# A hybrid attention block on one Trainium2 core: receptance of the first FFN from an input mixed beforehand, residual sums on GpSimd

## The chip, the core and the metric

The kernel runs on one core of a Trainium2 chip. The core has five engines that work side by side, each through its own queue of instructions in the order in which the program gave them: TensorE (PE in the profile, with PEld for the loading of its weights), VectorE (DVE), ScalarE (ACT), GpSimd (POOL) and SyncE (SP), which only issues transfers here. They wait for each other through semaphores. The metric is the device time of one execution in microseconds (us). The kernel before took 864.21 us in the median of three runs (862.68 to 866.72).

## The reference

The input x is (2, 2048, 128), all of it float32. Four parts follow each other, each as x = x + part(layernorm(x)): an attention, a feed-forward part (FFN), a linear attention with a decaying state, and the same FFN again. The change concerns the first FFN. Its computation, with C = 128 and the layernorm's output called x:

```
x_prev = concatenate([zeros, x[:, :-1, :]], axis=1)      # the token before
xr = mu_r * x + (1 - mu_r) * x_prev                      # mu_r, mu_k: one number per channel
xk = mu_k * x + (1 - mu_k) * x_prev
r  = sigmoid(xr @ W_r)                                   # receptance
k  = xk @ W_k
out = r * (square(relu(k)) @ W_v)
```

The result `out` is added to the stream that entered the layernorm.

## The kernel before

The stream X stays in SBUF through the whole kernel: 32 tiles of 128 tokens by 128 channels. The first FFN is the function `ffn_phase` (lines 775 to 984). It works on 8 groups of 4 tiles (512 tokens), which alternate between the two sequences of the batch. Group g of one sequence uses buffer `g.b`, so each tile has two buffers. Each engine runs a loop of its own over 10 slots (`run_slots`); `g.later(k)` is the group k places further on, and `exists` says whether there is one. The order inside `slot` is the order in which an engine's queue is filled. Nothing in it is reordered later. In slot g:

- VectorE: normalize group g+1 (four instructions, line 112), moments of group g+2 (line 94 and line 99), output of group g-2: `gated = (tanh + 1) * o` from PSUM (line 872) and then the residual sum into X (line 874).
- GpSimd: `low_part` of group g (line 848), the part of x that its rounded copy `x_hi` leaves out; then the inverse roots of group g+2 (lines 105 and 107), which the normalization of that group waits for.
- ScalarE: copy of the transposed x out of PSUM (line 904) and its rounded copy `x_hi` (line 906) for group g; then tanh (line 911), relu (line 916) and square (line 919) for group g-1. In slots 0, 1, 6 and 7 tables of the linear attention are computed there too.
- TensorE: transposes of group g (`turn`, line 947), receptance of group g-1 (lines 965 and 966), values of group g-2 (line 973), keys of group g-1 (lines 955 to 957).

After the transposition channels lie on the partitions, so "the token before" is the column to the left. `xT` has 1 + 512 columns, the first being the last one of the group before. The mixing with mu is not applied to x. It is in the weights: `FfnWeights.vector` makes two scaled copies of W_r and of W_k in the attention phase, and each product is done twice, once with x and once with x shifted by a column, into the same PSUM sum. The last FFN, which is woven into the end of the linear attention by another class (`LastFfn`), does the same and uses the same weights.

A `Block` ends when all engines have run through their part of it. The attention's block lies before the FFN's, the linear attention's behind it. In the last slots VectorE and GpSimd also compute the first normalization of the linear attention (`first_moments`, `first_gpsimd`, `first_normalized`).

Of the kernel before, what the change touches and what calls it, by code (L numbers as in the profile page):

```python
# [17 lines left out]
ALU = mybir.AluOpType  # L18
ACT = mybir.ActivationFunctionType
AX = mybir.AxisListType  # L20

P = 128
B, T, C = 2, 2048, 128
NT = T // P
GT = 4
G = GT * P
# [748 lines left out]
def ffn_phase(nc, X, const, weights, norm, name, out=None, tables=None, next_norm=None):  # L775


    normed = 2
    wr, wk_hi, wk_lo, wv = weights.wr, weights.wk_hi, weights.wk_lo, weights.wv
    ctx = ExitStack()  # L780
    with ctx:
        sb = lambda what, shape, dt=F32: ctx.enter_context(nc.sbuf_tensor(name + what, shape, dt))
# [4 lines left out]
        xT = sb("xT", [P, 2, 1 + G])  # L787
# [3 lines left out]
        k_act = sb("k_act", [P, 2, G])  # L791
        r_tanh = sb("r_tanh", [P, 2, G])
        gated = sb("gated", [P, 2, G])
        xt_ps = [psum(f"xt_ps{b}") for b in range(2)]
        k_ps = [psum(f"k_ps{b}") for b in range(2)]
        r_ps = [psum(f"r_ps{b}") for b in range(2)]
        o_ps = [psum(f"o_ps{b}") for b in range(2)]

        (set_up, xt_full, carried, xt_ready, hi_ready, lo_ready, k_full, k_pos_ready, k_act_ready, r_full, r_ready, o_full,
         gated_ready, x_ready, stored) = (sem(n) for n in (  # L800
             "set_up", "xt_full", "carried", "xt_ready", "hi_ready", "lo_ready", "k_full", "k_pos_ready", "k_act_ready",
             "r_full", "r_ready", "o_full", "gated_ready", "x_ready", "stored"))
        GROUPS = B * NG

        def run_slots(eng, slot):

            for k in range(GROUPS + 2):  # L810
                slot(Tile(0, k))

        AHEAD = 2

        def exists(g):
            return not isinstance(g.m, int) or 0 <= g.m < GROUPS

        def late(g):

            return not isinstance(g.m, int) or g.m >= 2  # L820

        def has_been_normed(g):
            return isinstance(g.m, int) and g.m < normed

        def tokens(g):
            return X[:, bass.ds(g.b * NT + g.n * GT, GT), :]
# [3 lines left out]
        @block.sync  # L830
        def _(eng):
            if tables is not None:
                tables.sync(eng)
            if out is not None:
                for k in range(GROUPS):
                    g = Tile(0, k)
                    eng.wait_ge(x_ready, k + 1)
                    eng.dma_start(out[g.b, g.n * G:(g.n + 1) * G, :].rearrange("(t p) c -> p t c", p=P),
                                  X[:, g.b * NT + g.n * GT:g.b * NT + (g.n + 1) * GT, :]).then_inc(stored, 16)
                eng.wait_ge(stored, 16 * GROUPS)  # L840

        @block.gpsimd
        def _(eng):
            eng.memset(xT[:, :, 0:1], 0.0).then_inc(set_up, 1)

            def low_part(g):
                eng.wait_ge(hi_ready, g.count(1, 1))
                eng.tensor_tensor(x_lo[:, g.b, :], xT[:, g.b, :], x_hi[:, g.b, :].bitcast(F32), ALU.subtract).then_inc(lo_ready, 1)

            def slot(g):  # L850
                if exists(g):
                    low_part(g)
                if exists(g.later(2)):
                    norm.inverse_roots(eng, g.later(2))
                if next_norm is not None and g.off == GROUPS - 2:
                    next_norm.first_gpsimd(eng)

            run_slots(eng, slot)

        @block.vector  # L860
        def _(eng):
            eng.sem_inc(gated_ready, AHEAD)

            def normalize(g):
                if late(g):
                    eng.wait_ge(xt_full, g.count(1, -1))
                norm.normalize(eng, g)

            def output(g):
                eng.wait_ge(r_ready, g.count(1, AHEAD + 1))  # L870
                eng.wait_ge(o_full, g.count(1, AHEAD + 1))
                eng.scalar_tensor_tensor(gated[:, g.b, :], r_tanh[:, g.b, :], 1.0, o_ps[g.b][:, :], ALU.add, ALU.mult).then_inc(gated_ready, 1)
                eng.wait_ge(gated_ready, g.count(1, AHEAD + 1))
                eng.tensor_tensor(tokens(g), gated[:, g.b, :].rearrange("p (t c) -> p t c", t=GT), tokens(g), ALU.add).then_inc(x_ready, 1)

            def slot(g):
                if next_norm is not None and g.off == GROUPS - 1:
                    next_norm.first_normalized(eng)
                if exists(g.later(1)) and not has_been_normed(g.later(1)):
                    normalize(g.later(1))  # L880
                if exists(g.later(2)):
                    norm.moments(eng, g.later(2))
                if exists(g.later(-2)):
                    output(g.later(-2))
                if next_norm is not None and g.off == GROUPS - 2:
                    eng.wait_ge(x_ready, B)
                    next_norm.first_moments(eng)

            run_slots(eng, slot)

        @block.scalar
        def _(eng):
            eng.sem_inc(r_ready, AHEAD)
            eng.sem_inc(k_pos_ready, AHEAD)
            eng.wait_ge(set_up, 1)
            def copy_x(g):
                eng.wait_ge(xt_full, g.count(1, 1))
                if late(g):

                    eng.wait_ge(k_full, g.count(1, -1))  # L900
                    eng.wait_ge(r_full, g.count(1, -1))
                    eng.activation(xT[:, g.b, 0:1], xT[:, g.b, G:G + 1], ACT.Copy).then_inc(carried, 1)
                    eng.wait_ge(carried, g.count(1, -1))
                eng.activation(xT[:, g.b, 1:1 + G], xt_ps[g.b][:, :], ACT.Copy).then_inc(xt_ready, 1)
                eng.wait_ge(xt_ready, g.count(1, 1))
                eng.activation(x_hi[:, g.b, :], xT[:, g.b, :], ACT.Copy).then_inc(hi_ready, 1)

            def tanh(g):
                eng.wait_ge(r_full, g.count(1, 1))
                eng.wait_ge(gated_ready, g.count(1, AHEAD - 1))  # L910
                eng.activation(r_tanh[:, g.b, :], r_ps[g.b][:, :], ACT.Tanh, scale=0.5).then_inc(r_ready, 1)

            def square(g):

                eng.wait_ge(k_full, g.count(1, 1))
                eng.activation(k_pos[:, g.b, :], k_ps[g.b][:, :], ACT.Relu).then_inc(k_pos_ready, 1)
                eng.wait_ge(k_pos_ready, g.count(1, AHEAD + 1))
                eng.wait_ge(o_full, g.count(1, AHEAD - 1))
                eng.activation(k_act[:, g.b, :], k_pos[:, g.b, :], ACT.Square).then_inc(k_act_ready, 1)

            def slot(g):
                if exists(g):
                    copy_x(g)
                if exists(g.later(-1)):
                    tanh(g.later(-1))
                    square(g.later(-1))
                if tables is not None and isinstance(g.m, int):
                    if g.m < 2:
                        tables.scalar_heads(eng, range(g.m * H // 2, (g.m + 1) * H // 2))
                    elif GROUPS - 2 <= g.m < GROUPS:  # L930
                        half = g.m - (GROUPS - 2)
                        tables.scalar_pairs(eng, range(half * NP // 2, (half + 1) * NP // 2))
                    elif g.m == GROUPS:
                        tables.scalar_rest(eng)

            run_slots(eng, slot)

        @block.tensor
        def _(eng):
# [18 lines left out]
                mm.then_inc(k_full, 1)  # L958

            def receptance(g):  # L960
                eng.wait_ge(xt_ready, g.count(1, 1))
                eng.wait_ge(r_ready, g.count(1, AHEAD - 1))
                for j in range(GT):
                    ps = r_ps[g.b][:, j * P:(j + 1) * P]
                    eng.matmul(ps, xT[:, g.b, 1 + j * P:1 + (j + 1) * P], wr[:, 0, :], start=True, stop=False)
                    mm = eng.matmul(ps, xT[:, g.b, j * P:(j + 1) * P], wr[:, 1, :], start=False, stop=True)
                mm.then_inc(r_full, 1)

            def values(g):
# [6 lines left out]
            def slot(g):  # L976
                if exists(g):
                    turn(g)
                if exists(g.later(-1)):
                    receptance(g.later(-1))  # L980
                if exists(g.later(-2)):
                    values(g.later(-2))
                if exists(g.later(-1)):
                    keys(g.later(-1))
# [1312 lines left out]
```

## Time and profile before

| | |
|---|---|
| median of three runs | 864.21 us (862.68 to 866.72) |
| the profiled execution's own time | 863.95 us |
| its span | 862.0 us, granted TensorE clock 0.984 |
| PE busy | 804.1 us (93%) |
| DVE busy | 550.2 us (64%) |
| ACT busy | 557.5 us (65%) |
| POOL busy | 562.2 us (65%) |
| first FFN's block in the trace | from 208.7 us to 252.2 us |

The span is the time between the first and the last instruction in the profile; the execution's own time is a little longer. A row of the timeline gives the start and the duration of one or several merged instructions, the engine, the line, the tile written and the tiles read. What stands in brackets is the time in which the engine was idle ahead of it and whom it waited for. The duration of an instruction that has started and can't proceed contains what it is held up.

### The profile page before, as it was taken

Reading aid. Unit: us, or ns where it says so; the run is one execution under the profiler, and the core shown is the slowest. Engines: PE = TensorE matmul, PEld = TensorE weight load, DVE = VectorE, ACT = ScalarE, POOL = GpSimd, SP = SyncE. Lnnn points to the kernel's source line nnn. Section 1 sums busy time; section 2 is a strip of 40 time slices with the busy share of each in tenths; the row PEclk is TensorE's granted clock in tenths of the full one; section 3 lists DMA queues with packets and bytes.
Section 4 is the critical chain, followed back from the end, with each engine's and each line's share of the span. In section 5 each row is a group of like instructions: output and inputs, shape, how many; then the busy total and the mean of one; then the engine's idle time right before and its main releaser. Section 6 shows DMA issues by size and latency. Waiting matters only on the chain.

```text
span 862.0 us, 31084 instructions
## 1 busy us (share of the span) xinstructions
PE 804.1 (93%) x13187; PEld 697.9 (81%) x13187; DVE 550.2 (64%) x1267; ACT 557.5 (65%) x1171; POOL 562.2 (65%) x449
## 2 busy tenths in 40 slices
PE   5879999998978999999999999999999999987886
PEld 4668998897967878888888878888788898786776
DVE  5997567566853665666666646656665667566573
ACT  5755555554768667677767766776777677754544
POOL 5961111214538888798797797797887977976431
PEclk9999999999989999999999999999999999998999
DMA  4300000100000000000000000000000000000011
GB/s 143 109 1 19 25 19 14 26 13 14 15 2 2 3 2 3 4 3 3 3 4 2 2 5 2 2 4 3 3 3 2 4 3 2 5 3 2 14 37 49
DMA packets 20423, 12.36 MB, mean 14 GB/s; under 512 B 7872, under 2 KB 19008, under 8 KB 20288
## 3 DMA queue, kind: packets, MB, share of 16 engines
q1 hardware_dynamic: 20288, 10.39, 4.3%
q8 instruction: 105, 1.72, 0.8%
q14 instruction: 30, 0.25, 0.1%
HBM read 8.29 MB, written 2.10 MB: 12 GB/s over the span
## 4 chain that ended last, share of the span: by engine, by line
PE 52%; ACT 6%; POOL 5%; DVE 4%; issue 3%; ACTq 0%; POOLq 0%; DVEq 0%
PE la_ps L1465 8%; PE la_ps L1467 6%; PE la_ps L1466 6%; PE la_o_ps L1528 4%; PE la_o_ps L1544 4%; PE la_s_ps L1558 4%; PE la_ps L1575 3%; PE la_ps L1509 3%; ACT la_u_hi L1960 2%; PE la_ps L1496 2%; PE la_ps L1610 2%; PE la_ps L1611 2%; PE la_ps L1612 2%; ACT n_xn L2000 2%; POOL la_scale L2151 1%
## 5 line engine op out<-in xcount | busy, mean ns | idle before, releaser
L2119 POOL TENSOR_TENSOR la_coef<-la_ssk,lt_mhalf 128x32 f32<-128x32 f32 x16 | 87.0, 5440 | 72.3 <-DVE la_ssk L1788 72.3
L1465 PE MATMUL la_ps<-la_x_hi,w_hi 128*128 128x256 f32 x384 | 116.8, 304 | 2.0 <-ACT la_v L1930 1.0
L1466 PE MATMUL la_ps<-la_x_lo,w_hi 128*128 128x256 f32 x384 | 107.6, 280 | 0.2 <-issue 0.2
L1467 PE MATMUL la_ps<-la_x_hi,w_lo 128*128 128x256 f32 x384 | 107.7, 280 | 0.0
L2151 POOL TENSOR_TENSOR la_scale<-la_scale,lt_mhalf 128x32 f32<-128x32 f32 x16 | 97.8, 6110 | 5.3 <-DVE la_scale L1764 5.2
L1811 DVE TENSOR_TENSOR lt_state<-la_s_ps,la_faded 128x512 f32<-128x512 f32 x62 | 42.6, 687 | 69.9 <-PE la_o_ps L1544 46.5
L1465 PEld LDWEIGHTS la_ps<-la_x_hi,w_hi 128*128 128x128 f32 x384 | 72.2, 188 | 14.3 <-issue 6.2
L524 POOL CAST w_hi<-qkv_w_raw 128x256 fp32r<-128x256 f32 x20 | 7.9, 396 | 115.0 <-PE qkv_xt_ps L566 78.9
L593 PE MATMUL qkv_v_ps<-V,qkv_probsT 128*128 128x128 f32 x544 | 72.0, 279 | 2.6 <-DVE qkv_probsT L507 1.6
L593 PEld LDWEIGHTS qkv_v_ps<-V,qkv_probsT 128*128 128x128 f32 x544 | 67.9, 192 | 7.4 <-ACT qkv_probsT L697 2.5
L1466 PEld LDWEIGHTS la_ps<-la_x_lo,w_hi 128*128 128x128 f32 x384 | 72.5, 189 | 0.8 <-issue 0.4
L1467 PEld LDWEIGHTS la_ps<-la_x_hi,w_lo 128*128 128x128 f32 x384 | 72.3, 188 | 0.0
L1951 ACT ACTIVATE la_gate<-la_ps,lt_bias_g 128x256 f32<-128x256 f32 x128 | 50.0, 482 | 33.1 <-PE la_ps L1467 33.1
L2145 POOL TENSOR_TENSOR la_faded<-lt_state,lt_decay_s 128x512 f32<-128x512 f32 x62 | 64.1, 1043 | 2.2 <-DVE lt_state L1811 2.2
L1748 DVE TENSOR_TENSOR la_pT<-la_ps,lt_decay 128x512 f32<-128x512 f32 x64 | 41.0, 683 | 38.1 <-PE la_ps L1509 38.1
L2137 POOL TENSOR_TENSOR la_k<-la_k,lt_decay_k 128x1024 f32<-128x1024 f32 x32 | 60.9, 1904 | 2.0 <-issue 1.1
L2129 POOL TENSOR_TENSOR la_v<-la_v,la_coef 128x1024 f32<-128x1024 f32 x32 | 60.2, 1903 | 1.3
L1951 ACT ACTIVATE la_f<-la_ps,lt_bias_f 128x256 f32<-128x256 f32 x128 | 51.5, 472 | 14.7 <-PE la_ps L1467 13.3
L689 ACT ACTIVATE qkv_probs<-qkv_xt_ps,at_ntop 128x512 f32<-128x512 f32 (+3 forms) x48 | 30.4, 633 | 46.8 <-DVE at_ntop L630 46.8
L1465 PE MATMUL la_ps<-w_hi,la_x_hi 128*128 128x512 f32 x128 | 57.4, 448 | 0.0
L1930 ACT ACTIVATE la_k<-la_ps 128x512 f32<-128x512 f32 x64 | 38.3, 598 | 26.3 <-PE la_ps L1467 23.3
L1544 PE MATMUL la_o_ps<-la_qdT,lt_state 64*64 64x64 f32 x2048 | 46.1, 224 | 8.4 <-issue 5.0
(225 smaller groups left out, 2439.3 us busy)
## 6 DMA issues: line engine op xcount, KB each, us to landing
qkv_w_raw<-in_w SPq DMA_DIRECT2D x20, 128.0 KB, 2.2
X<-in_x SPq DMA_DIRECT2D x8, 256.0 KB, 2.9
out<-X SPq DMA_DIRECT2D x8, 256.0 KB, 2.3
qkv_cos<-in_cos SPq DMA_DIRECT2D x4, 256.0 KB, 3.1
qkv_sin<-in_sin SPq DMA_DIRECT2D x4, 256.0 KB, 3.9
lt_w_out<-in_w_out SPq DMA_DIRECT2D x4, 128.0 KB, 2.7
qkv_w<-in_w_qkv SPq DMA_DIRECT2D x1, 320.0 KB, 3.2
const<-in_const SPq DMA_DIRECT2D x1, 256.5 KB, 5.3
```

The source lines that it names most:

```text
L593: mm = eng.matmul(o_ps[n % 2][:, 0:P], probsT[:, (BLK[n] + j) % 2, t * P:(t + 1) * P], V[:, bass.ds(b * NT + kt, 1), :], start=(kt == 0), ...
L1465: eng.matmul(out, l_hi, r_hi, start=True, stop=False)
L1466: eng.matmul(out, l_hi, r_lo, start=False, stop=False)
L1467: return eng.matmul(out, l_lo, r_hi, start=False, stop=True)
L1544: mm = eng.matmul(o_ps[h % 2][rows, part(i, c)], state[own, b, h // 2, :], qdT[own, b, h // 2, chunk(c)], start=False, stop=True, skip_gro ...
L1811: eng.tensor_tensor(state[:, b, :, :], s_ps[c][:, :].rearrange("p (r e) -> p r e", r=NP), faded[:, b, :, :], ALU.add).then_inc(up_read[c], 1)
L1951: act = eng.activation(where[:, c, :], ps[bank][:, r * W:(r + 1) * W], ACT.Tanh, bias=bias[:, c:c + 1], scale=0.5)
L2119: eng.tensor_tensor(coef[:, :], ssk[:, :], mhalf[:, :], ALU.pow).then_inc(s["coef_step"], 1)
L2129: eng.tensor_tensor(own, own, over_d(coef[:, b * H:(b + 1) * H]), ALU.mult).then_inc(s["vb_ready"], 1)
L2137: eng.tensor_tensor(own, own, over_d(decay_k[:, :]), ALU.mult).then_inc(s["kd_ready"], 1)
L2145: eng.tensor_tensor(faded[:, b, :, :], state[:, b, :, :], over_e, ALU.mult).then_inc(s["faded_second" if c else "faded_first"], 1)
L2151: eng.tensor_tensor(scale[:, :, :], scale[:, :, :], powers, ALU.pow).then_inc(s["scale_step"], 1)
```

## The change

The receptance gets its mixed input, `xr = mu_r * x + (1 - mu_r) * x_prev`, computed ahead of the product. ScalarE multiplies x by mu_r with one more instruction per group (`own_ready`), and VectorE adds the shifted x times (1 - mu_r) with one `scalar_tensor_tensor` (`mix`, between the normalization and the moments of a slot). TensorE then does the receptance's product once, with the unscaled weights. The residual sum moves from VectorE's `output` to the end of GpSimd's slot (`residual`), and `output` waits until the residual sum two groups back has read `gated`. The last FFN stays as it is.

```diff
-    wr, wk_hi, wk_lo, wv = weights.wr, weights.wk_hi, weights.wk_lo, weights.wv
+    wk_hi, wk_lo, wv = weights.wk_hi, weights.wk_lo, weights.wv
...
+        xr = sb("xr", [P, 2, G])
...
+            def residual(g):
+                eng.wait_ge(gated_ready, g.count(1, AHEAD + 1))
+                eng.tensor_tensor(tokens(g), gated[:, g.b, :].rearrange("p (t c) -> p t c", t=GT), tokens(g), ALU.add).then_inc(x_ready, 1)
+
             def slot(g):
                 if exists(g):
                     low_part(g)
                 if exists(g.later(2)):
                     norm.inverse_roots(eng, g.later(2))
+                if exists(g.later(-2)):
+                    residual(g.later(-2))
                 if next_norm is not None and g.off == GROUPS - 2:
                     next_norm.first_gpsimd(eng)
...
             def output(g):
                 eng.wait_ge(r_ready, g.count(1, AHEAD + 1))
                 eng.wait_ge(o_full, g.count(1, AHEAD + 1))
+                if late(g):
+                    eng.wait_ge(x_ready, g.count(1, -1))
                 eng.scalar_tensor_tensor(gated[:, g.b, :], r_tanh[:, g.b, :], 1.0, o_ps[g.b][:, :], ALU.add, ALU.mult).then_inc(gated_ready, 1)
-                eng.wait_ge(gated_ready, g.count(1, AHEAD + 1))
-                eng.tensor_tensor(tokens(g), gated[:, g.b, :].rearrange("p (t c) -> p t c", t=GT), tokens(g), ALU.add).then_inc(x_ready, 1)
+
+            def mix(g):
+
+                own = xr[:, g.b, :]
+                eng.wait_ge(own_ready, g.count(1, 1))
+                eng.scalar_tensor_tensor(own, xT[:, g.b, 0:G], weights.rest[:, 0:1], own, ALU.mult, ALU.add).then_inc(xr_ready, 1)
 
             def slot(g):
                 if next_norm is not None and g.off == GROUPS - 1:
                     next_norm.first_normalized(eng)
                 if exists(g.later(1)) and not has_been_normed(g.later(1)):
                     normalize(g.later(1))
+                if exists(g):
+                    mix(g)
                 if exists(g.later(2)):
                     norm.moments(eng, g.later(2))
                 if exists(g.later(-2)):
...
                 eng.activation(x_hi[:, g.b, :], xT[:, g.b, :], ACT.Copy).then_inc(hi_ready, 1)
+                eng.activation(xr[:, g.b, :], xT[:, g.b, 1:1 + G], ACT.Copy, scale=weights.mu[:, 0:1]).then_inc(own_ready, 1)
...
             def receptance(g):
-                eng.wait_ge(xt_ready, g.count(1, 1))
+                eng.wait_ge(xr_ready, g.count(1, 1))
                 eng.wait_ge(r_ready, g.count(1, AHEAD - 1))
                 for j in range(GT):
-                    ps = r_ps[g.b][:, j * P:(j + 1) * P]
-                    eng.matmul(ps, xT[:, g.b, 1 + j * P:1 + (j + 1) * P], wr[:, 0, :], start=True, stop=False)
-                    mm = eng.matmul(ps, xT[:, g.b, j * P:(j + 1) * P], wr[:, 1, :], start=False, stop=True)
+                    part = slice(j * P, (j + 1) * P)
+                    mm = eng.matmul(r_ps[g.b][:, part], xr[:, g.b, part], weights.w[:, 0, :], start=True, stop=True)
                 mm.then_inc(r_full, 1)
```

## Rows read from the trace of the kernel before

**Rows 1.** The page, busy time by engine over the span
```profile
PE 804.1 (93%) x13187; PEld 697.9 (81%) x13187; DVE 550.2 (64%) x1267; ACT 557.5 (65%) x1171; POOL 562.2 (65%) x449
```
**Rows 2.** Timeline, PE: first transposes, then one slot (start us, duration us)
```profile
208.86 1.07 PE L947 MATMUL f_xt_ps<-const,n_xn 128*128 128x128 f32 x8 [0.87 <-PEq L147]
...
229.52 0.79 PE L947 MATMUL f_xt_ps<-const,n_xn 128*128 128x128 f32 x4
230.15 0.40 PE L965 MATMUL f_r_ps<-fw_wr,f_xT 128*128 128x128 f32 x2
...
231.95 1.06 PE L973 MATMUL f_o_ps<-fw_wv,f_k_act 128*128 128x128 f32 x8
...
234.22 0.77 PE L947 MATMUL f_xt_ps<-const,n_xn 128*128 128x128 f32 x4
```
**Rows 3.** Timeline, VectorE in the same slot
```profile
227.89 2.04 DVE L112 TENSOR_SCALAR n_xn<-X,n_mv,n_rstd 128x128 f32<-128x128 f32 x4 [0.17 <-POOL n_rstd L107]
229.85 0.86 DVE L94 BATCH_NORM_STATS2 n_stats<-X 128x6 f32<-128x128 f32 x4
...
231.74 0.69 DVE L874 TENSOR_TENSOR X<-f_gated,X 128x512 f32<-128x512 f32 x1
232.60 2.00 DVE L112 TENSOR_SCALAR n_xn<-X,n_mv,n_rstd 128x128 f32<-128x128 f32 x4 [0.17 <-POOL n_rstd L107]
```
**Rows 4.** Timeline, GpSimd in the same slot
```profile
227.79 1.29 POOL L848 TENSOR_TENSOR f_x_lo<-f_xT,f_x_hi 128x513 fp32r<-128x513 f32 x1
231.21 0.20 POOL L105 TENSOR_TENSOR n_rstd<-n_mv,n_eps 128x4 f32<-128x4 f32 x1 [2.13 <-DVE n_mv L99]
231.49 1.01 POOL L107 TENSOR_TENSOR n_rstd<-n_rstd,n_mhalf 128x4 f32<-128x4 f32 x1
232.46 1.29 POOL L848 TENSOR_TENSOR f_x_lo<-f_xT,f_x_hi 128x513 fp32r<-128x513 f32 x1
```
**Rows 5.** Timeline, the first and the last of the slot's four normalizing instructions
```profile
227.89 1.27 DVE L112 TENSOR_SCALAR n_xn<-X,n_mv,n_rstd 128x128 f32<-128x128 f32 x1 [0.17 <-POOL n_rstd L107]
...
229.59 0.34 DVE L112 TENSOR_SCALAR n_xn<-X,n_mv,n_rstd 128x128 f32<-128x128 f32 x1
```
**Rows 6.** Groups by line between 206 and 258 us: receptance, first product
```profile
L965 PE MATMUL f_r_ps<-fw_wr,f_xT 128*128 128x128 f32 x64 | 12.5, 278 | 0.3 <-ACT f_xT L904 0.3
```
**Rows 7.** Timeline, ScalarE: the rounded copy, and the wait for the keys
```profile
231.73 0.63 ACT L906 ACTIVATE f_x_hi<-f_xT 128x513 fp32r<-128x513 f32 x1
...
234.42 0.60 ACT L916 ACTIVATE f_k_pos<-f_k_ps 128x512 f32<-128x512 f32 x1 [1.56 <-PE f_k_ps L957]
```
**Rows 8.** Timeline, attention stage: GpSimd and VectorE, all with two SBUF inputs
```profile
52.70 1.29 POOL L254 TENSOR_TENSOR qkv_rot<-qkv_by_cos,qkv_by_sin 128x512 f32<-128x512 f32 x1
53.95 1.75 POOL L254 TENSOR_TENSOR qkv_rot<-qkv_by_cos,qkv_by_sin 128x512 f32<-128x512 f32 x1
...
52.73 1.81 DVE L298 TENSOR_TENSOR qk_lo<-qkv_rot,qk_hi 128x512 fp32r<-128x512 f32 x1
```
**Rows 9.** Timeline, GpSimd at the start of the first FFN
```profile
210.94 1.28 POOL L848 TENSOR_TENSOR f_x_lo<-f_xT,f_x_hi 128x513 fp32r<-128x513 f32 x1 [2.17 <-ACT f_x_hi L906]
...
212.46 1.03 POOL L107 TENSOR_TENSOR n_rstd<-n_rstd,n_mhalf 128x4 f32<-128x4 f32 x1
```
**Rows 10.** Timeline, the first FFN's end: VectorE, then PE
```profile
243.38 1.55 DVE L112 TENSOR_SCALAR n_xn<-X,n_mv,n_rstd 128x128 f32<-128x128 f32 x2 [0.33 <-POOL n_rstd L107]
...
251.19 0.69 DVE L874 TENSOR_TENSOR X<-f_gated,X 128x512 f32<-128x512 f32 x1
...
247.45 0.40 PE L957 MATMUL f_k_ps<-f_x_lo,fw_wk_hi 128*128 128x512 f32 x1
...
249.20 1.16 PE L973 MATMUL f_o_ps<-fw_wv,f_k_act 128*128 128x128 f32 x8 [1.35 <-ACT f_k_act L919]
```
**Rows 11.** Windows: stretch, PE, PEld, DVE, ACT, POOL busy us, then the granted clock
```profile
56.00:60.00 4.00, 1.99 (x12) 1.47 (x12) 3.79 (x12) 1.58 (x5) 2.41 (x2) 1.00 0.00 0
60.00:64.00 4.00, 3.34 (x15) 3.06 (x16) 3.79 (x14) 2.70 (x8) 0.00 (x0) 0.57 0.02 4
```

More of the change, by code:

```diff
@@ L797, in ffn_phase @@
         o_ps = [psum(f"o_ps{b}") for b in range(2)]
-        (set_up, xt_full, carried, xt_ready, hi_ready, lo_ready, k_full, k_pos_ready, k_act_ready, r_full, r_ready, o_full,
+        (own_ready, xr_ready, set_up, xt_full, carried, xt_ready, hi_ready, lo_ready, k_full, k_pos_ready, k_act_ready, r_full, r_ready, o_full,
          gated_ready, x_ready, stored) = (sem(n) for n in (
-             "set_up", "xt_full", "carried", "xt_ready", "hi_ready", "lo_ready", "k_full", "k_pos_ready", "k_act_ready",
+             "own_ready", "xr_ready", "set_up", "xt_full", "carried", "xt_ready", "hi_ready", "lo_ready", "k_full", "k_pos_ready", "k_act_ready",
              "r_full", "r_ready", "o_full", "gated_ready", "x_ready", "stored"))
```

## The prediction

> **What bounds the kernel now.** The page comes first: PE is busy for 93% of the span, the other engines for about 65% [rows 1]. Taken alone that says "PE bound", and the change takes PE work away. So the question for the first FFN is whether PE sets its pace there. I read the timeline of one slot, engine by engine, and look at which end a start follows.
>
> On PE a slot lasts from 229.52 to 234.22, 4.70 us, without idle time [rows 2]. Of that the receptance takes 231.95 - 230.15 = 1.80 us, values and keys 234.22 - 231.95 = 2.27 us, and the four transposes 230.15 - 229.52 = 0.63 us. Eight unhindered transposes took 1.07 us, of which the last one's duration is about 0.27, so one follows another after (1.07 - 0.27)/7 = 0.114 us and four need 0.46 us [rows 2]. The slot's transposes are therefore stretched by 0.17 us: they are waiting for something. The last normalizing instruction ends at 229.59 + 0.34 = 229.93 [rows 5], and the receptance starts 0.22 us behind it. A busy PE hides a wait of its own.
>
> What VectorE waits for is in [rows 3, 4]. It goes round in a loop with GpSimd, which needs nobody else:
> - the roots of a group end at 227.79 (GpSimd's next instruction starts there);
> - normalization 227.89 to 229.93. Unhindered it would be four instructions at 0.26 us. But GpSimd started `low_part` at 227.79 and VectorE's first instruction is held until this has nearly ended: 1.27 us instead of 0.34 [rows 5];
> - moments 229.85 to 231.13, roots 231.21 to 231.49 + 1.01 = 232.50, and VectorE starts on the next group at 232.60.
> From 227.79 to 232.50 is 4.71 us, the same as PE's slot, with only the short handovers between the engines in it. So the pace is set by this loop; PE, with 4.07 + 0.46 = 4.53 us of work, is close behind. The old residual sum (0.69 us) lies beside the roots [rows 3, 4], off the loop.
>
> **The change, part by part.**
> *Removed from PE.* Line 965 has 64 instructions in the eight groups, line 966 as many; a slot's receptance goes from 1.80 to 0.90 us, 7.2 us in all [rows 2, 6]. In the steady slots it is worth at most nothing, since the loop does not contain PE. It would count where PE is the path, in the tail (below).
> *Added on ScalarE.* One 128x512 copy with a scale; the nearest row is the rounded copy, 0.63 us, after which the next instruction starts 0.54 us on. ScalarE is idle for 1.56 us per slot waiting for the keys [rows 7], which hides it: 0, at worst 0.54 us a slot. It delays tanh, relu and the squares of the group before, for which PE has time once it is no longer close to the bound.
> *Moved off VectorE.* The residual sum, 0.69 us beside the roots: 0 on the loop.
> *Added on VectorE.* `mix` stands between normalization and moments, so it is on the loop. The nearest row for 128x512 with two SBUF inputs is 0.69 us [rows 3]; as the next instruction starts 0.60 us after it, I take 0.60. Bounds: 0.54 (the copy's step on ScalarE) and 1.81, the same shape held by a GpSimd instruction [rows 8]. The unhindered one is the nearer, as GpSimd has run out of streaming work when `mix` comes.
> *Added on GpSimd.* The residual sum of group g-2 stands right behind the roots of g+2 and ahead of `low_part` of g+1. Nearest rows: 1.29 us for the same size [rows 4, 8]. Its input is ready, because `output` runs beside the roots. So GpSimd starts it the moment the roots end, while VectorE starts 0.10 us later and finds it running. Two streaming instructions of GpSimd now come one after the other where there was one, and normalization has to wait for both. How they take turns is in [rows 8]: VectorE's 52.73 instruction was held by GpSimd's 52.70, ran when that ended, and GpSimd's next (53.95) was held for 1.75 - 1.29 = 0.46 us. So one normalizing instruction gets in between the two.
>
> *Sum of the loop.* 4.71 + 1.25 (residual sum) + 0.15 (the second GpSimd instruction held by a normalizing one) - 0.26 (that one is done already) + 0.60 (mix) = 6.45 us; if none gets in between, 4.71 + 1.28 + 0.60 = 6.59. I take 6.5, +1.8 per slot. Residual sums exist from slot 2 on. Before that a slot costs 4.71 + 0.60 = 5.3.
>
> The trace and the Trainium skill (SBUF — State Buffer, Who interferes with whom) can be weighed here. It says that the shared port pair is held for a whole instruction and that the loser blocks fully. By that a normalization held at 227.89 would end a full 0.34 + 3 x 0.26 = 1.12 us after `low_part`'s 229.08, at 230.20; the row says 229.93. With the page's version two collisions of 0.27 us a slot would come on top, about 2 us in all. The measurement decides; the sum goes by the rows. Another sentence of that section agrees with rows 8 and speaks against `mix`: a VectorE instruction with two SBUF inputs collides too.
>
> *Start.* `mix` of group 0 now stands ahead of the moments of group 2. It waits for ScalarE's two copies and is then held by `low_part` (210.94 + 1.28 = 212.2 [rows 9]): ends 212.8, moments 214.0, roots 215.35, against 212.46 + 1.03 = 213.5 before: +1.9. Roots of group 3: 215.35 + 5.3 = 220.7; group 4: 226.0; then 6.5 each: group 5 at 232.5, group 6 at 239.0, group 7 at 245.5. Before, group 7's were at 237.2 (232.50 and one more slot of 4.7). That is +8.3.
>
> *Tail.* Normalization of group 7 ends 3.3 instead of 2.1 us behind its roots: +9.5, at 248.8. Then mix, output and the linear attention's first moments on VectorE (the residual sum's 0.6 gone, mix's 0.6 added), but their roots must pass the residual sum of group 4 on GpSimd, some 0.6 us: the last first-normalized tile, before at 243.38 + 1.55 = 244.93 [rows 10], comes at 255.0. `mix` of group 7 is queued behind it, 255.6, and only now can PE do receptance, values and keys: 0.90 + 2.27 + 0.15 = 3.3 us, 258.9 instead of 247.45 + 0.40 = 247.85. That is +11.0; here PE's saved 0.90 us is already counted. From there relu, square, values and output as before, and a residual sum of 1.29 instead of 0.69 us [rows 10]: +11.6.
>
> *The clock.* PE now rests about 3 us per slot (6.5 - 3.6), in one piece, behind its keys. In the attention stage a window with 1.99 of 4 us busy was followed by one at granted clock 0.57 [rows 11], that is, most of it at the lower level of 1.2 GHz. In the steady slots PE has room for half speed over some 3.5 us. In the tail it hasn't: keys of group 6 end at about 252.7, PE then rests until 255.6, and the 3.3 us behind it may be done at half speed for most of their length: bounds 0 and +3.3, I take 1.3. Nothing behind the first FFN changes; its block starts as late as this one ends.
>
> Total: 11.6 + 1.3 = +12.9 us. The profiled execution took 863.95 us, 0.26 under the median, so 876.8 by its own time and **877.0 us** against the median.
>
> **The rivals.**
> *A: PE sets the pace.* For it: no idle time in the slot [rows 2] and 93% [rows 1]. Then 8 x 0.90 = 7.2 us go: 857. Against: the stretched transposes and the 0.22 us behind normalization in each slot.
> *B, not slower: the collisions don't add up.* If GpSimd's two streaming instructions ran beside the moments and beside VectorE's waits, the loop would be 0.10 + 1.03 + 0.60 + 1.28 + 0.08 + 1.29 = 4.4 us, 0.3 under today's. Six slots give -1.8, the receptance in the tail up to -1.8, the start +1.2 and the longer last sum +0.6: about 862.5. It decides if the residual sum is released later than the start of normalization. For it: the order of queueing between two engines is only read from rows of another stage. Against: `gated` is ready 0.8 us before the roots end.
> *C: only one of the two collides.* VectorE, once it has the port, gets all four and mix through ahead of `low_part`: 1.25 + 1.03 + 0.60 + 1.28 + 0.08 + 1.29 = 5.5 us per slot. The last three slots are 1.0 shorter each and the tail about 1: 873.
> *D: the clock makes PE the bound.* At half speed throughout, a slot's 3.6 us of PE become 7.3 (6.5 before): +0.8 x 4 slots and the tail's 3.3 in full: 882. Against: a PE that is busy throughout doesn't lose its clock [rows 11].
>
> **How the numbers follow.** The forecast has 0.55, C 0.20, D 0.10, A 0.05, B 0.10. The forecast's own range is 873 to 880; with C and D it is 869 to 882, which leaves out A, B and a rest. A measurement of this kernel can tell about 0.5% (4.3 us) from no change. Slower by more than that (above 868.5): forecast, C and D, 0.85. Within: B, and a rest of C, 0.10 less the part of B that goes further down, taken as 0.09. Faster: A and that part, 0.06.
>
> **What would show it.** In the profile after: the distance between two inverse roots (line 107 of `n_rstd`) in the middle of the first FFN is 6.4 to 6.6 us (forecast), 5.5 (C), 4.4 (B) or below 4.0 (A). The first normalizing instruction of a slot lasts about 1.3 us, and the second one too. GpSimd's residual sum starts within 0.1 us of the roots' end. PE shows 3 us idle a slot, with the clock at times at 0.5, and DVE as the releaser of the receptance. The block ends at about 265 instead of 252. It would be wrong if roots came at an even 4.7 us or less, or if the stages behind the first FFN took another time than before.

## The result, and the profile after

The changed kernel takes 880.8 us in the median of four runs (880.06 to 882.02), the kernel before 864.36 us beside it: ratio 1.0189, 95% interval 1.0167 to 1.021, or 16.4 us slower. The forecast was 877.0. The profiled execution took 880.06 us, its span is 878.0.

The loop of VectorE and GpSimd that stands in [rows 3, 4] comes first, since the forecast rests on it. GpSimd in the changed kernel, one slot and the next one's start:

```profile
226.57 1.28 POOL L853 TENSOR_TENSOR X<-f_gated,X 128x512 f32<-128x512 f32 x1
227.81 1.27 POOL L849 TENSOR_TENSOR f_x_lo<-f_xT,f_x_hi 128x513 fp32r<-128x513 f32 x1
231.62 0.20 POOL L105 TENSOR_TENSOR n_rstd<-n_mv,n_eps 128x4 f32<-128x4 f32 x1 [2.54 <-DVE n_mv L99]
231.90 1.02 POOL L107 TENSOR_TENSOR n_rstd<-n_rstd,n_mhalf 128x4 f32<-128x4 f32 x1
232.89 1.27 POOL L853 TENSOR_TENSOR X<-f_gated,X 128x512 f32<-128x512 f32 x1
```

And VectorE in the same slot, each normalizing instruction by itself; the last row is `mix`:

```profile
226.71 1.22 DVE L112 TENSOR_SCALAR n_xn<-X,n_mv,n_rstd 128x128 f32<-128x128 f32 x1 [0.90 <-POOL n_rstd L107]
227.86 1.31 DVE L112 TENSOR_SCALAR n_xn<-X,n_mv,n_rstd 128x128 f32<-128x128 f32 x1
229.09 0.34 DVE L112 TENSOR_SCALAR n_xn<-X,n_mv,n_rstd 128x128 f32<-128x128 f32 x1
229.34 0.33 DVE L112 TENSOR_SCALAR n_xn<-X,n_mv,n_rstd 128x128 f32<-128x128 f32 x1
229.60 0.74 DVE L887 SCALAR_TENSOR_TENSOR f_xr<-f_xT,fw_rest,f_xr 128x512 f32<-128x512 f32 x1
```

The residual sum starts the moment the roots end, the first normalizing instruction 0.14 us later is held by it until 227.93, and the second one is held by `low_part` until 229.17. In [rows 5] only the first was held. From one start of the residual sum to the next (226.57 to 232.89) it is 6.32 us, against 4.71 before.

PE in that slot; before, this stretch had no gap at all [rows 2]:

```profile
228.08 0.30 PE L963 MATMUL f_xt_ps<-const,n_xn 128*128 128x128 f32 x1 [0.54 <-DVE n_xn L112]
229.22 0.84 PE L963 MATMUL f_xt_ps<-const,n_xn 128*128 128x128 f32 x3 [0.84 <-DVE n_xn L112]
230.40 1.16 PE L981 MATMUL f_r_ps<-fw_w,f_xr 128*128 128x128 f32 x8 [0.33 <-DVE f_xr L887]
```

Together PE rests for 1.71 us of the slot, in three pieces, and part of its wait is hidden in the transposes, which take longer than where they run free.

The first FFN's start and end. The start: `mix` of group 0 on VectorE (1.25 us, held by `low_part`) and the receptance that waited for it. The end: the last residual sum, and ScalarE's first instruction in the linear attention's block:

```profile
211.59 1.25 DVE L887 SCALAR_TENSOR_TENSOR f_xr<-f_xT,fw_rest,f_xr 128x512 f32<-128x512 f32 x1 [3.11 <-ACT f_xr L922]
```

```profile
212.90 2.08 PE L981 MATMUL f_r_ps<-fw_w,f_xr 128*128 128x128 f32 x8 [2.88 <-DVE f_xr L887]
...
262.47 1.26 POOL L853 TENSOR_TENSOR X<-f_gated,X 128x512 f32<-128x512 f32 x1 [2.62 <-DVE f_gated L881]
...
264.05 1.28 ACT L2092 ACT_TABLE_LOAD   x1 [2.89 <-PEq L781]
```

I take as the block's length the time from GpSimd's first instruction in it (208.77 here, 208.68 before) to this table load (264.05, before 252.16): 55.28 us against 43.48, +11.8. What lies behind it, up to the span's end, is 878.0 - 264.05 = 614.0 us against 862.0 - 252.16 = 609.8, +4.1. Nothing was edited there.

The clock at the start, in 1 us windows (us, busy PE, PEld, DVE, ACT, POOL, granted clock, share and rate of the transfers):

```profile
212.00:213.00 1.00, 0.10 (x1) 0.10 (x1) 1.00 (x3) 1.00 (x6) 0.30 (x1) 0.62 0.34 43
213.00:214.00 1.00, 1.00 (x5) 1.00 (x6) 0.96 (x9) 0.97 (x4) 0.00 (x0) 0.50 0.39 83
```

PE had rested for 2.88 us waiting for `mix`; then it worked at 1.2 GHz until 219. PE was at that level twice more before 260 us: the granted clock is 0.57 between 236 and 240 us and 0.60 between 250 and 254.

### The profile page after: what moved, and what is told of

It reads as the page before. It is cut to its first block, busy times and chain, and to the rows that moved or that the text cites. A ratio compares the mean times of both kernels' runs of the same rounds, so it can differ in the third digit from the quotient of the medians.

```text
span 878.0 us, 30972 instructions
## 1 busy us (share of the span) xinstructions
PE 807.9 (92%) x13123; PEld 698.6 (80%) x13123; DVE 554.3 (63%) x1267; ACT 564.1 (64%) x1179; POOL 574.8 (65%) x457
## 4 chain that ended last, share of the span: by engine, by line
PE 49%; ACT 7%; POOL 6%; DVE 4%; issue 4%; ACTq 0%; POOLq 0%; DVEq 0%
PE la_ps L1480 8%; PE la_ps L1482 6%; PE la_ps L1481 6%; PE la_o_ps L1559 4%; PE la_o_ps L1543 4%; PE la_s_ps L1573 4%; PE la_ps L1590 3%; PE la_ps L1524 3%; ACT la_u_hi L1975 3%; PE la_ps L1511 2%; ACT n_xn L2015 2%; PE la_ps L1625 2%; PE la_ps L1626 2%; PE la_ps L1627 2%; POOL la_scale L2166 1%
```

## The experiments

Each was compared with the kernel before on its own chip. "Roots" is the distance between the ends of two inverse roots in the middle of the first FFN. "Behind" the block is what lies between its end and the end of the span. Both come from the one profiled execution of each kernel, while the times of several executions of a kernel lie 1 to 8 us apart.

**The parts one by one.** e1: the mixing alone.

```diff
-                if exists(g.later(-2)):
-                    residual(g.later(-2))          # GpSimd's slot
...
+                eng.wait_ge(gated_ready, g.count(1, AHEAD + 1))      # VectorE's output
+                eng.tensor_tensor(tokens(g), gated[...], tokens(g), ALU.add).then_inc(x_ready, 1)
```

> The changed kernel with the residual sum back on VectorE, behind the output: the mixing alone. Theory (the loop VectorE-GpSimd sets the pace; mix adds its 0.66 us step to it, no second collision): distance of two inverse roots in the middle of the first FFN 4.71 + 0.66 = 5.37 us, the FFN's block 7.0 us longer than before, 871.4 us. Rival A (PE sets the pace, so its 7.2 us come back when GpSimd's sum is gone): distance 4.0 or less, 858 us. Rival 'the sum on GpSimd is the whole loss': 864.

Measured: 877.56 us against 863.9, ratio 1.0156 (1.0133 to 1.018). Roots 5.33 us, block 51.97 us (+8.5, of which 3.5 lie behind the last roots), behind the block 615.0. The chain of GpSimd, two slots apart:

```profile
230.26 1.01 POOL L107 TENSOR_TENSOR n_rstd<-n_rstd,n_mhalf 128x4 f32<-128x4 f32 x1
...
235.59 1.01 POOL L107 TENSOR_TENSOR n_rstd<-n_rstd,n_mhalf 128x4 f32<-128x4 f32 x1
```

So PE's saved work does not come back in the loop, and mix costs its step there. The total missed the forecast by 6 us: 1.5 in the block, and 5 behind it.

e2: the moved sum alone, `residual` on GpSimd in the kernel before.

```diff
+                if exists(g.later(-2)):
+                    residual(g.later(-2))          # behind inverse_roots
...
```

> The kernel before with nothing but the residual sum moved to the end of GpSimd's slot. Theory: no mix, but every normalization from group 4 on is held by two GpSimd instructions, +0.97 us (the changed kernel's 2.97 against 2.00): distance 5.7 us, three or four such slots, and 0.6 us more in the last sum: block 4.5 us longer, 869 us. Rival 'a moved sum is free, mix is the whole loss': 865 (its longer duration at the end alone). Rival B (no collision): distance 4.7.

Measured: 869.42 us, ratio 1.0067 (1.0051 to 1.0083). Roots 5.66, block 47.99 (+4.5), behind it 610.8. VectorE's normalization, four instructions merged:

```profile
229.63 2.98 DVE L112 TENSOR_SCALAR n_xn<-X,n_mv,n_rstd 128x128 f32<-128x128 f32 x4 [0.91 <-POOL n_rstd L107]
```

As expected in every number: 2.98 instead of 2.04 us [rows 3]. The parts add up roughly: 8.5 + 4.5 = 13.0 against the changed kernel's 11.8 in the block.

e3: the changed kernel with `mix` beside the roots.

```diff
-                if exists(g):
-                    mix(g)                          # behind normalize
...
                 if exists(g.later(-2)):
                     output(g.later(-2))
+                if exists(g):
+                    mix(g)
```

> The changed kernel with mix moved behind the output in VectorE's slot, so it lies beside the inverse roots as the residual sum once did. Theory of the first FFN: the loop loses mix's 0.66 us, distance of the roots 5.66 us as with the sum alone; block 49.8 us, 6.3 more than before (the receptance of group 7 now waits for output and mix). Rival (mix costs nothing where it stands, the collisions are all): distance stays 6.3. On the linear attention behind it: theory Q (TensorE's queue, shorter by 64 passes, meets its slow places elsewhere) 614 to 615 us and 874.7 us in all; rival (nothing but chance there) 610 and 870.5.

Measured: 878.53 us, ratio 1.0169 (1.0148 to 1.019). Roots 5.66, so mix's 0.66 us is gone from the loop. But the block is 52.81, 3 us longer than expected: the tail behind the last roots, where the last mix now stands behind an output, grew to 20.5 us. Behind the block 615.1.

**Does PE set the pace?** e6: half the receptance left out of the kernel before.

```diff
-                    eng.matmul(ps, xT[:, g.b, 1 + j * P:1 + (j + 1) * P], wr[:, 0, :], start=True, stop=False)
-                    mm = eng.matmul(ps, xT[:, g.b, j * P:(j + 1) * P], wr[:, 1, :], start=False, stop=True)
+                    mm = eng.matmul(ps, xT[:, g.b, 1 + j * P:1 + (j + 1) * P], wr[:, 0, :], start=True, stop=True)
```

> The kernel before with the second of the receptance's two products left out (the token before is missing from r): PE has 0.9 us less per slot and nothing else changes. Theory: distance of the inverse roots stays at 4.7, PE gets idle time of about 0.7 us a slot, and only the receptances of groups 6 and 7 behind the last normalization are worth something: 1.8 us, 862.6. Rival A (PE sets the pace): distance 3.8 and 857.

Measured: roots 4.67, block 42.22 (-1.3). PE visibly waits for the normalization in every steady slot now, which it did before too, only unseen:

```profile
229.80 1.01 PE L947 MATMUL f_xt_ps<-const,n_xn 128*128 128x128 f32 x4 [0.47 <-DVE n_xn L112]
```

Rival A is out: 0.9 us of PE's work less per slot moved the pace by nothing. The median of ten runs is 866.36 us, 2.5 more than before (1.0027, 1.0013 to 1.0041), although the block is shorter and nothing was added anywhere; 862.6 was expected. It has to come from behind the block, but the profile of e6 does not show it in its length (609.9 us): the profiled execution took 863.42 us, the fastest of the ten.

e4: the collision taken away in the kernel before.

```diff
             def low_part(g):
                 eng.wait_ge(hi_ready, g.count(1, 1))
+                if exists(g.later(1)):
+                    eng.wait_ge(norm.ready, g.count(GT, 2 * GT))
```

> The kernel before, in which low_part of group g on GpSimd also waits until VectorE has normalized group g+1, so it runs beside the moments instead of holding the normalization. Theory: the loop falls to 3.85 us, PE with 4.53 us of work becomes the bound: distance 4.53 to 4.6, each normalizing instruction 0.33 us; block 1 us shorter, 863.4, no more. Rival A (PE is the bound already): nothing changes, 864.4, or later by low_part's delay.

Measured: 861.67 us against 863.9, ratio 0.998 (0.9965 to 0.9996); block 41.49 (-2.0), behind it 609.5. The normalization takes 1.12 us instead of 2.04, and `low_part` follows it:

```profile
225.63 1.12 DVE L112 TENSOR_SCALAR n_xn<-X,n_mv,n_rstd 128x128 f32<-128x128 f32 x4 [0.28 <-POOL n_rstd L107]
```

```profile
226.89 1.30 POOL L850 TENSOR_TENSOR f_x_lo<-f_xT,f_x_hi 128x513 fp32r<-128x513 f32 x1 [1.37 <-DVE n_xn L112]
```

PE's slot became 4.51 us, as the 4.53 of work said. The roots themselves run at 3.9, ahead of PE, which the expectation had put at PE's pace. The gain is twice the expected one. PE's rows say where it comes from: counted from the block's start, the transposes of group 2 begin at 10.35 us instead of 11.30, since PE no longer waits for group 1's held normalization (0.89 us before), and the last transposes begin at 28.41 instead of 30.22. So one microsecond comes at the start, which the expectation had left out, and the rest from the shorter slots.

**Can the mixing be had for nothing?** e5: e1, e3 and e4 together.

> The changed kernel with three things mended: residual sum back on VectorE, mix behind it, and low_part of group g held until group g+1 is normalized. Theory: nothing of the added work is on the loop (3.85 us), VectorE's own work (1.03 + 1.20 + 0.60 + 0.60 + 0.66 = 4.1 us) becomes the bound: distance 4.1 to 4.2, block 40 us, 3.5 under before. In all 862 to 865 with theory Q (the linear attention 2 to 4.5 us longer as TensorE's queue is shorter), 860.5 with the rival (chance).

Measured: 873.59 us, ratio 1.0122 (1.0098 to 1.0145), block 49.8 instead of 40, behind it 615.5 (in an execution of 876.73 us, 3 us over the median). The theory of e5 was wrong. The roots came at 3.9 to 6.5 us, and the waits between 212 and 259 us say why:

```profile
PE f_r_ps L977 <- DVE f_xr L883: 11.9, 7, 2.9
ACT f_k_pos L928 <- PE f_k_ps L969: 8.4, 6, 3.1
```

The mixing makes a ring of its own. Receptance waits for `mix`, values and keys are queued behind the receptance, ScalarE's relu and square wait for the keys, and the next copy of x, from which `mix` is made, is queued behind those. Before, the receptance waited for ScalarE's first copy only. That the slower loop hides this ring in the changed kernel is argued from the waits; no run takes the ring apart.

**The 4 us behind the block.** The kernels with a longer rest (after, e1, e3, e5, and by its median e6) have one thing in common: TensorE's queue is shorter ahead of the linear attention, by 128 instructions (32 products of two passes, each with a weight load). e7: the changed kernel with the product issued twice.

```diff
+                    for _ in range(2):
                         mm = eng.matmul(r_ps[g.b][:, part], xr[:, g.b, part], weights.w[:, 0, :], start=True, stop=True)
```

> The changed kernel whose single receptance product is issued twice with the same operands, so TensorE has the same number of instructions ahead of the linear attention as before the change. First FFN: 0.9 us more PE work per slot in PE's idle time, so the block is 55 us as in the changed kernel, 1 us more in the tail. Theory Q: the linear attention is back to 609.5 to 611 us, in all 877.5. Rival (chance, or the clock): 614 as in the changed kernel, 881.5.

Measured: 876.82 us, ratio 1.0153 (1.013 to 1.0175). The block is 1.3 us longer than the changed kernel's (56.56), the kernel is 4 us faster (3.1 by the ratios, as the two ran on different chips); behind the block 610.7.

e8: e5 with 32 small products behind the second transposes.

```diff
+                if g.m == 1:
+                    for _ in range(4 * GROUPS):
+                        eng.matmul(r_ps[1][:, 0:4], ident, weights.w[:, 0, 0:4], start=True, stop=True)
```

> e5 with 32 small products (four columns, into a part of PSUM that the receptance overwrites) in PE's idle time behind the second transposes, so TensorE's instruction count ahead of the linear attention is that of before. First FFN: block 40 to 40.5 us. Theory Q: the linear attention 609.5 to 611, 860.5 in all, and 2 to 4 us less than e5. Rival (chance): same as e5.

Measured: 877.16 us, ratio 1.0152 (1.0132 to 1.0172). The pads were no pads: their 64 passes took 11.3 us (210.51 to 221.77), and the block became 57.35. The first 24 follow each other in 0.11 us, the other 40, at a granted clock of 0.50, in 0.21 us. That is what passes of 128 columns take in the same profile, 0.11 us at the full clock and 0.21 at half.

Behind the block it took 608.6 us, 7 less than in e5's profile; the medians without the blocks differ by 4.0 (873.59 - 49.80 = 823.8 and 877.16 - 57.35 = 819.8). So the total was missed and the part in question came out as theory Q had it.

e9 and e10 change the number of repetitions: `range(2 if g.m < 4 else 1)` and `range(3)`.

> The changed kernel with the receptance product issued twice for the first four groups alone: TensorE has 64 instructions fewer ahead of the linear attention than before the change (the changed kernel has 128 fewer, e7 none). First FFN: block 55.3 us as in the changed kernel. Theory Q (what stands ahead in TensorE's queue decides where in the linear attention it stalls): its length is neither fixed to 610 nor to 614 and may be anything between; if the effect is simply 'fewer is slower', 612.3 us, in all 879. Rival (the pads of e7 worked through the block's timing, not the count): 610.5 as e7.

> The changed kernel with the product issued three times: 128 instructions more ahead of the linear attention than before the change. First FFN: PE work 5.4 us in a slot of 6.3, block 57 us. 'Fewer is slower': linear attention 606 us, in all 874. Theory Q by position (a stall comes where the queue is refilled, which moves with the count and comes round again): not monotonic, 608 to 615, in all 876 to 883.

Measured: e9 879.78 us (1.0179, 1.0154 to 1.0204), block 56.65, behind it 611.3; e10 881.71 us (1.0193, 1.0165 to 1.0221), block 59.15, behind it 611.9. Both blocks are longer than expected (55.3 and 57): 7.3 and 7.9 us between the roots of groups 3 and 4, near the cold start. "Fewer is slower" falls with e10.

What the count does shows in the steps of the linear attention. In each profile I took the start of the sixteen `la_coef` instructions and the span's end, counted from the block's end, and subtracted the same of the kernel before (us; in front, TensorE's instructions ahead compared with before):

```
-128 after  0.1  0.9 -0.2  1.4  1.4  2.5  4.0  2.6  1.6  2.1  2.1  1.3  2.2  2.7  1.7  2.7 | 4.2
-128 e1     0.8  0.8 -0.4  0.9  0.9  2.1  3.6  2.2  1.0  1.9  2.1  1.4  2.0  3.4  2.7  5.0 | 5.2
-128 e3     0.6  0.6 -0.5  0.5  0.7  1.2  3.1  1.8  0.5  1.1  1.5  1.0  1.9  3.1  2.0  4.5 | 5.3
-128 e5     1.1  1.1  0.0  1.6  1.8  2.6  4.5  3.3  2.1  2.1  2.0  1.2  2.1  2.9  1.8  3.5 | 5.7
-128 e6     0.0  0.0 -1.2 -0.1 -0.2  0.8  1.7  0.3 -0.7 -0.2 -0.1 -0.7 -0.7  0.3 -0.3  1.6 | 0.1
 -64 e9     0.8  0.8 -0.3 -0.1  0.4  0.6  2.1  2.0  0.8  0.3 -0.3 -0.4 -0.1  0.7  0.7  0.7 | 1.5
   0 e2     0.4  0.4 -1.6 -1.4 -0.7 -0.5  0.2  0.0  0.2  0.4  0.3  0.3  0.1 -0.2 -0.2 -0.1 | 0.9
   0 e4     1.1  1.1 -0.9 -1.1 -0.7 -0.8 -0.4 -0.1  0.1 -0.5 -0.6 -0.6 -0.3 -0.6 -0.4 -0.1 |-0.3
   0 e7     0.4  1.0 -1.1 -0.8 -0.9 -0.7 -0.3 -0.2 -0.3 -0.5 -0.2 -0.7 -0.7 -0.7 -0.7 -0.1 | 0.9
   0 e8     0.8  0.8 -0.3 -0.4  0.0 -0.3  0.0 -0.4 -0.8 -1.3 -1.3 -0.6 -0.6 -0.8 -1.1 -1.1 |-1.2
   0 e11    0.6  0.6 -0.5 -0.5  0.4  0.7  0.8  0.9  0.5  0.3  0.6  0.5  0.3  0.3  0.3  0.3 | 1.5
+128 e10    0.9  1.1  0.0  1.0  1.3  2.1  3.5  2.4  1.2  1.8  1.7  1.0  1.6  2.8  1.8  3.7 | 2.1
```

The five kernels with 128 fewer have quite different first FFNs and the same curve, with its hump at the seventh step (e6's lies lower); the five with the count of before have no hump; and +128 has the curve of -128, with a smaller sum at the end. The blocks' lengths, 41.1 to 59.2 us, play no part in it. Nor does the clock: between the third step (73 us behind the block) and the fifteenth (477 us) it is 1.00 in every profile.

The last column is one execution each and moves by some 1.5 us by chance (-1.2 to 1.5 at an unchanged count). The medians less the block are steadier: 819.8 to 821.4 us with the count of before (before itself, e2, e4, e7, e8, e11), 823.8 to 825.7 with 128 fewer (after 825.5, e1 825.6, e3 825.7, e5 823.8, e6 824.1), 823.1 with 64 fewer and 822.6 with 128 more (on their chip the kernel before has 821.3). Here e6 falls in line, in which nothing but TensorE's count was changed.

TensorE's own rows show what moves. At one and the same pass, the 3207th behind the block, it pauses in all five kernels with 128 fewer (changed kernel 1.15 us, e1 1.15, e3 0.60, e5 0.88, e6 0.88) and in e10 (0.83), and in none of the other seven. Four more places behave alike. The place in the kernel before, in the changed kernel and in e10:

```profile
412.35 0.67 PE L1544 MATMUL la_o_ps<-la_qdT,lt_state 64*64 64x64 f32 x32
```

```profile
426.94 0.57 PE L1559 MATMUL la_o_ps<-la_qdT,lt_state 64*64 64x64 f32 x22 [1.15 <-issue]
```

```profile
430.35 0.57 PE L1560 MATMUL la_o_ps<-la_qdT,lt_state 64*64 64x64 f32 x22 [0.83 <-issue]
```

"issue" is time in which the engine waited for nothing that the profile shows. Every kernel has 11 to 17 such pauses behind the block, 6 to 9 us in all, and neither number goes with the count (before 7.0 us, after 7.7). What goes with the count is where they fall. So it is shown that the rest of the kernel depends on how many TensorE instructions stand ahead of it. Why the pauses come, that their places cost the 4 us, and that the pattern comes round again after 256 instructions (only -128 and +128 say so) are not shown.

**A kernel that beats both.** e11: e4 with the last group's keys first on TensorE, and its square ahead of its tanh on ScalarE.

```diff
...
+                last = g.m == GROUPS
+                if last:
+                    keys(g.later(-1))
                 if exists(g.later(-1)):
                     receptance(g.later(-1))
...
-                if exists(g.later(-1)):
+                if exists(g.later(-1)) and not last:
                     keys(g.later(-1))
```

> Meant as the better kernel: e4 (the kernel before with low_part held until the normalization is through) in which the last group's keys go ahead of its receptance and of the values of group 6 on TensorE, and its square ahead of its tanh on ScalarE. Theory: the block's end hangs on keys, relu, square, values, output; 1.80 + 0.81 us leave that path and receptance fills the wait for the square: block 39 to 40 us against e4's 41.5 and 43.5 before; TensorE's count is unchanged, so the linear attention stays at 609.5 to 610.5; 859.5 in all. Rival (the tail hangs on the first moments and the output of group 6): no gain over e4, 861.5.

Measured: 861.65 us against 864.75, ratio 0.9965 (0.9947 to 0.9984), 3.1 us faster than before. It missed the expected 859.5 us and block of 39 to 40, and came out as its rival had it: against e4 it is a draw, block 41.13 instead of 41.49. The keys of group 7 now wait for `low_part`, and two outputs with their sums stand one behind the other on VectorE at the end, from 246.89 to 248.90:

```profile
241.71 0.50 PE L961 MATMUL f_k_ps<-f_x_hi,fw_wk_hi 128*128 128x512 f32 x1 [0.53 <-POOL f_x_lo L850]
```

## Why the prediction was right, and where it was off

The direction and the mechanism in the first FFN were right. The total, 880.8 us, lies above the forecast's own range of 873 to 880, and inside 869 to 882 only because that adds C and D, which did not happen. A stage that the forecast took as unchanged made the difference.

*The bound.* Right, and shown: e6 takes PE's work away and the pace stays at 4.67 us; e4 takes the collision away and PE's slot falls from 4.70 to 4.51.

*mix on the loop, 0.60 us.* Right. Its step is 0.66 (229.60 to the moments' 230.26); e1 shows it in the roots, 5.33 against 4.71.

*The two GpSimd instructions in a row.* Right in mechanism, e2 shows it alone. The way of taking turns was off: the forecast had one normalizing instruction gone by before the second GpSimd instruction, and the latter held for 0.15 us. In fact GpSimd is not held at all (1.27 us), and the one that gets in between ends only 0.09 us behind `low_part`. Normalization takes 2.97 us, not 3.3, and the loop 6.32, not 6.5.

*The Trainium skill's whole-instruction lock* (SBUF — State Buffer, Who interferes with whom): the rows of the changed kernel side against the extra 0.27 us again. The first normalizing instruction ends at 227.93, 0.08 us behind the residual sum's 227.85. That the loser waits nearly to the end agrees.

*Start.* Nearly right: roots of group 2 end at 215.44 (forecast 215.35), those of group 3 at 220.80 (220.7). The roots of group 4 came at 226.60 instead of 226.0: PE had lost its clock before, group 2's copies came late, and mix waited for ScalarE for 0.76 us; that the clock made them late is read from the rows and not tested. The smaller step of 6.32 made up for it by luck: group 7's roots end at 245.57, forecast 245.5.

*Tail and clock.* The tail came step by step as forecast: the last first-normalized tile at 254.93 (255.0), `mix` of group 7 at 255.60 (255.6), the last keys at 259.10 (258.9). The block ends at 264.05; 252.16 + 11.6 = 263.8 was forecast ahead of the clock's 1.3 us. The term for the clock should have been nothing: PE did fall to half speed at 250 us, but in the receptance and the values of groups 6 and 5, for which nobody waited, and had the full clock back at 254, before the last keys. The rest that the term was built on was too long: not 3 us in one piece but 1.71 us in three in a steady slot, and 1.23 instead of 2.9 us ahead of the last receptance. So the first FFN was forecast at +12.9 and measured at +11.8.

*"Nothing behind the first FFN changes; its block starts as late as this one ends."* This is the step that failed. +4.1 us in the profile came from there, a quarter of the loss; with the other terms' errors (-1.1) it makes nearly the whole difference between 877.0 and 880.8. The prediction had named such a change behind the first FFN as a sign that it would be wrong, and put the term at nothing without a row for it. e7 shows that TensorE's count is behind it: with the count restored the changed kernel needs 610.7 us there, and is 3 to 4 us faster in all with a longer block. Why the count matters stays open.

*Rivals.* A is out by e6. B is out: the sum starts within 0.03 us of the roots' end. C is out: two normalizing instructions are held, not one. D did not come about: PE lost its clock for some slots and had it back by itself, and the roots kept their 6.32 us. The reason given against D does not stand in [rows 11]: they show the fall behind a stretch with rests, and nothing of a PE without them.

## What to carry to other kernels

An engine that is busy for the whole of a slot need not set the pace: look at what the start of its work follows, and whether any of its instructions is longer than where it runs free. Before work is moved to GpSimd, look at which VectorE instruction stands at the same place in time; where GpSimd streams through SBUF beside a VectorE instruction that collides, one wait that shifts it by an instruction (e4) may be worth more than work taken away. And where a change alters how many instructions TensorE has, compare the untouched stages as well: here they moved by 4 us.

## What the runs showed of the hardware that was not expected

- Passes with only four columns follow each other at the pace of passes with 128, each with its weight load: 0.11 us at the full clock, 0.21 us at half (e8). 64 of them, issued in PE's rest, took 11.26 us: a small product is no cheap filler.
- A copy with a scale read from SBUF takes 0.71 us on ScalarE (line 922), the plain one of nearly the same size (line 921) 0.63.
- The time of the linear attention depends on the number of TensorE instructions ahead of it. In single profiles it took 608.6 to 611.3 us with the count of before (before, e2, e4, e7, e8, e11), 614.0 to 615.5 with 128 fewer (after, e1, e3, e5; e6's fastest execution 609.9), 611.3 with 64 fewer and 611.9 with 128 more. The pauses of TensorE without a releaser stand at the same five places in all kernels with -128 and +128, and at none of these in the others.
